# Attention over six nodes: the value product in two column halves, projections in the gap between them, the q edge folded into Wq, the residual summed in PSUM

## The reference, cut to what matters

```python
for c in range(NUM_NOD):                       # 6 nodes, D = 128, H = 8 heads of 16
    nsrc = min(c + 1, MAX_PREV)
    snode = c - nsrc
    eq, ek, ev = (lind + nsrc - 1, lind, lind + nsrc // 2)
    in_q, in_k, in_v = (c - 1, snode, snode + nsrc // 2)
    q = ew[c, 0] * (nodes[in_q] @ We[eq] + be[eq])
    k = ew[c, 1] * (nodes[in_k] @ We[ek] + be[ek])
    v = ew[c, 2] * (nodes[in_v] @ We[ev] + be[ev])
    o = _mha(q, k, v, Wq[c], Wk[c], Wv[c], Wo[c])   # softmax((q Wq)(k Wk)^T / 4) (v Wv) Wo
    nodes[c] = act_w[c] * o + q
    lind += nsrc
out = nodes[NUM_NOD - 1]
return _layernorm(out, ln_g, ln_b)
```

## Time and profile before

| what | value |
|---|---|
| runs shown | 2585.63, 2601.75 and 2603.72 us, median 2601.75 |
| the profiled execution | 2587.72 us, of which the span of the trace is 2585.9 |
| PE busy | 2319.4 us, 90% |
| DVE busy | 2235.8 us, 86% |
| ACT busy | 1781.2 us, 69% |
| mean granted TensorE clock | 0.959 |

### The profile page before, as it was taken

The page is one execution under the profiler, slowest core; times in us unless marked ns, Lnnn a source line. Parts: engine busy times, 40 slices in busy tenths (PEclk is TensorE's granted clock), DMA queues, the critical chain, the costliest instruction groups (busy, mean ns, idle before and its releaser), DMA issues.

```text
span 2585.9 us, 39227 instructions
## 1 busy us (share of the span) xinstructions
PE 2319.4 (90%) x13473; PEld 869.1 (34%) x13473; DVE 2235.8 (86%) x3998; ACT 1781.2 (69%) x3417; POOL 115.0 (4%) x74
## 2 busy tenths in 40 slices
PE   6588989999999999999999999999999999999996
PEld 3233333333333333333333333333333333333331
DVE  7488788899989999899999999999899899898982
ACT  3136567777777777777777777777777777767773
POOL 1000000000000000000000000000000000010110
PEclk8679899999999999999999999999999999999995
DMA  3404133242253243253243243243243243143311
GB/s 90 108 21 83 39 74 79 54 115 77 60 114 75 62 114 76 61 115 80 58 114 81 57 105 85 46 105 83 47 105 87 44 105 89 42 104 88 65 29 33
DMA packets 93262, 198.46 MB, mean 77 GB/s; under 512 B 26115, under 2 KB 43799, under 8 KB 93063
## 3 DMA queue, kind: packets, MB, share of 16 engines
q1 hardware_dynamic: 93062, 195.96, 32.4%
HBM read 116.65 MB, written 64.42 MB: 70 GB/s over the span
## 4 chain that ended last, share of the span: by engine, by line
PE 63%; DVE 14%; ACT 11%; DMA 6%; issue 4%; SPq 2%; ACTq 0%; POOL 0%; POOLq 0%; DVEq 0%
PE bank L511 25%; PE bank L464 22%; ACT e_ring L670 10%; DVE max_half L963 9%; PE bank L484 5%; DMA q_aug<-max_part 5%; PE bank L312 2%; PE bank L323 2%; PE bank L342 2%; SPq L1167 2%; PE bank L331 1%; PE bank L257 1%; PE bank L350 1%; ACT raw L680 1%; PE bank L258 1%
## 5 line engine op out<-in xcount | busy, mean ns | idle before, releaser
L963 DVE TENSOR_REDUCE max_half<-bank 128x1 f32<-128x512 f32 x3072 | 1924.3, 682 | 257.1 <-PE bank L484 243.4
L670 ACT ACTIVATE e_ring<-bank 128x512 f32<-128x512 f32 x3072 | 1610.9, 601 | 609.7 <-PE bank L464 609.4
L464 PE MATMUL bank<-q_aug,k_aug 50*128 50x512 f32 x3072 | 1142.0, 453 | 159.0 <-ACT e_ring L670 149.7
L484 PE MATMUL bank<-k_aug,q_aug 48*128 48x512 f32 x3072 | 1153.0, 456 | 48.2 <-DMA q_aug<-part_dram 25.7
L464 PEld LDWEIGHTS bank<-q_aug,k_aug 50*128 50x128 f32 x3072 | 503.2, 188 | 1209.9 <-ACT e_ring L670 1113.0
L511 PE MATMUL bank<-e_ring,v_aug 128*32 128x512 f32 x6144 | 836.7, 617 | 0.0
L484 PEld LDWEIGHTS bank<-k_aug,q_aug 48*128 48x128 f32 x3072 | 500.8, 188 | 84.9 <-DVE max_half L963 49.6
L511 PEld LDWEIGHTS bank<-e_ring,v_aug 128*32 128x32 f32 x6144 | 121.7, 108 | 206.4 <-ACT e_ring L670 117.9
L1030 POOL TENSOR_TENSOR ctxT<-ctxT,rden_bc 128x1024 f32<-128x1024 f32 x23 | 54.6, 2375 | 1938.9 <-DMA rden_bc<-rden_dram 1938.8
L680 ACT ACTIVATE raw<-bank 128x512 f32<-128x512 f32 x96 | 57.4, 598 | 27.9 <-PE bank L511 26.0
L331 PE MATMUL bank<-node_ring,w_q 128*128 128x512 f32 x96 | 56.2, 670 | 3.1 <-DVE k_part L805 0.7
(11 more groups left out here) (167 smaller groups left out, 687.8 us busy)
## 6 DMA issues: line engine op xcount, KB each, us to landing
part_dram<-k_part SPq DMA_DIRECT2D x24, 1024.0 KB, 4.0
k_aug<-part_dram SPq DMA_DIRECT2D x48, 512.0 KB, 10.1
part_dram<-q_part SPq DMA_DIRECT2D x24, 1024.0 KB, 5.0
q_aug<-part_dram SPq DMA_DIRECT2D x48, 512.0 KB, 13.4
src<-node_dram SPq DMA_DIRECT2D x40, 512.0 KB, 3.4
k_aug<-part_dram SPq DMA_DIRECT2D x48, 256.0 KB, 8.1
q_aug<-part_dram SPq DMA_DIRECT2D x48, 256.0 KB, 14.4
q_aug<-max_part SPq DMA_DIRECT2D x768, 2.0 KB
```

Of the source, the lines that this page charges most:

```text
L464: e.matmul(bank[i][:, :], k_aug[first:first + AUG, u % 2, h // 2, chunk * P:(chunk + 1) * P].bitcast(F32R), q_aug[first:first + AUG, u % 2 ...
L484: e.matmul(bank[i][:, :], q_aug[first:first + SPLIT, u % 2, h // 2, q0:q0 + P].bitcast(F32R), k_aug[first:first + SPLIT, u % 2, h // 2, ha ...
L670: e.activation(e_ring[:, n % E_SLOTS, :], bank[i][:, :], ACT.Exp, scale=EXP_SCALE).then_inc(a_exp, 1)
L963: e.tensor_reduce(max_half[:, G % 2, row, kh:kh + 1], bank[MAX_BANKS[ring % 3]][:, :], AX_X, ALU.max).then_inc(v_mx, 1)
```

## The change

- **Value product.** In a step in which PE has no side product, the value product is issued in two halves of 256 columns: the first before the last pair of score and maxima products, the second after it. In a step with a side product, that product takes the place ahead of the last pair and the value product stays whole, at the end.
- **Side products.** At most one in a step. `project_q` is gone: We[eq] is folded into Wq in the prologue (`fold`), and qh comes straight from the node. Each output projection now begins with the edge product of the node (`project_node`, accumulated in bank 7), and `project_out` adds Wo's product on top, so PE does 10 in a unit again, at r = 0, 1 (qh), 4, 5 (kh), 12 to 15 (node and output, twice) and 24, 25 (v). ACT evicts the sum with one bias (`evict_out`); DVE's `add_out` is gone. The bias of v is carried through Wo (`out_biases`), so DVE's eviction of v is a plain copy.
- **Parts of q and k.** ACT evicts the unrounded value, and POOL rounds it and subtracts (`split`, two instructions of 128x512 each, four times a unit). DVE's `rest_k` and `rest_q` are gone.
- **Maxima.** The transpose moves from r % 8 = 2 to r % 8 = 3 and from the ring of maxima banks to bank 7; DVE's negation follows at the end of that step.
- **SP.** The order of the list within a unit changes: q's store and loads come first (r = 3, 5, 6), k's store and loads after the denominators (r = 7, 9, 10), and the source of v moves from r = 23 to r = 11.

```diff
+        QH_AT, KH_AT, OUT_AT, TURN_AT, V_AT = (0, 1), (4, 5), (12, 13, 14, 15), (16, 17), (24, 25)
...
             def head_q(u, hf, at):
                 c, b = divmod(u, B)
                 where["qh", u, hf] = at
                 bk = free_bank(at)
-                e.wait_ge(a_q, 2 * u + hf + 1)
-                e.matmul(bk[:, :], w_q[:, c, :], node_ring[:, b, (c + 1) % 2, half_of(hf)], start=True, stop=True).then_inc(p_qh, 1)
-                freed[at] = (v_qr, 2 * u + hf + 1)
+                wait_node(u)
+                e.matmul(bk[:, :], w_q[:, c, :], node_ring[:, b, c % 2, half_of(hf)], start=True, stop=True).then_inc(p_qh, 1)
+                freed[at] = (a_q1, 2 * u + hf + 1)
...
+            def project_node(u, hf):
+
+                c, b = divmod(u, B)
+                bk = free_bank(MISC)
+                e.matmul(bk[:, :], w_edge_q[:, c, :], node_ring[:, b, c % 2, half_of(hf)], start=True, stop=False)
+
             def project_out(u, hf):
                 c, b = divmod(u, B)
-                bk = free_bank(MISC)
                 e.wait_ge(g_norm, u + 1)
-                e.matmul(bk[:, :], w_o[:, c, :], ctxT[:, half_of(hf)], start=True, stop=True).then_inc(p_o, 1)
-                freed[MISC] = (v_oa, 2 * u + hf + 1)
+                e.matmul(bank[MISC][:, :], w_o[:, c, :], ctxT[:, half_of(hf)], start=False, stop=True).then_inc(p_o, 1)
+                freed[MISC] = (a_oa, 2 * u + hf + 1)
...
+            def turn_maxima(G):
+                bk = free_bank(MISC)
+                e.wait_ge(v_cmb, G + 1)
+                e.transpose(bk[0:NR, 0:P], max_col[:, G % 2, :], ident[:, :]).then_inc(p_turn, 1)
+                freed[MISC] = (v_neg, G + 1)
+
+            def weighted(z, columns, first, last):
...
+                if first:
+                    e.wait_ge(a_exp, HG * z + HG)
...
+                for j in range(HG):
+                    done = e.matmul(bank[CTX_BANK][j * VW:(j + 1) * VW, columns], v_aug[:, u % 2, chunk, hg * HG + j, :],
+                                    e_ring[:, (HG * z + j) % E_SLOTS, columns], start=(chunk == 0 and first),
+                                    stop=(chunk == NCH - 1 and last))
+                if last:
+                    done.then_inc(p_ctx, 1)
...
             for s in range(-LOOKAHEAD, LAST_STEP):
+                product = product_of(s)
+                late = late_stages(s)
+                z = s - 1
                 for j in range(HG):
...
+                    if j == HG - 1:
+                        if product:
+                            product()
+                        elif 0 <= z < STEPS:
+                            weighted(z, slice(0, BANK // 2), True, False)
                     if 0 <= s < STEPS:
...
+                        scores(s, j)
...
+                        maxima(m)
                 if 0 <= z < STEPS:
...
+                    if product:
+                        weighted(z, slice(0, BANK), True, True)
+                    else:
+                        weighted(z, slice(BANK // 2, BANK), False, True)
+                for i, k in late:
+                    mix(i, k, lambda: MISC)
...
+            def evict_out(u, hf):
...
+                e.activation(node_ring[:, b, (c + 1) % 2, half_of(hf)], bank[MISC][:, :], ACT.Identity,
+                             bias=col[:, C_BO + c:C_BO + c + 1]).then_inc(a_oa, 1)
...
+            def split(part, hf, signal_to):
+                x, high = part[:, 1, half_of(hf)], part[:, 0, half_of(hf)]
+                after()
+                step(e.tensor_copy(high.bitcast(F32R), x))
+                after()
+                signal(e.tensor_tensor(x, x, high, ALU.subtract), signal_to)
...
             def store_k(u):
-                e.wait_ge(v_kr, 2 * u + 2)
+                e.wait_ge(g_k, 2 * u + 2)
...
             def store_q(u):
-                e.wait_ge(v_qr, 2 * u + 2)
+                e.wait_ge(g_q, 2 * u + 2)
...
                     if 1 <= nxt < UNITS:
-                        k = r - shift_of(nxt)
                         if r == 0:
                             load_source(nxt, 0)
-                        if k == 6:
+                        if r == 3:
+                            store_q(nxt)
+                        if r in (5, 6):
+                            load_aug(nxt, 0, r - 5)
+                        if r == 7:
                             store_k(nxt)
-                        if k == 8:
-                            store_q(nxt)
-                        if k in (8, 9):
-                            load_aug(nxt, 1, k - 8)
-                        if k in (11, 12):
-                            load_aug(nxt, 0, k - 11)
-                        if r == 23:
+                        if r in (9, 10):
+                            load_aug(nxt, 1, r - 9)
+                        if r == 11:
                             load_source(nxt, 1)
```

More of the change, by code:

```diff
@@ L304, in wait_node @@
                 else:
[L305 to L313, removed]
+                    e.wait_ge(a_oa, 2 * (u - B) + 2)
             def head_k(u, hf, at):
@@ L370, in last_turn, with scores @@
                 freed[MISC] = (a_last, hf + 1)
-            def stages(s, half):
+            def scores(s, j):
+                n = HG * s + j
+                G, chunk = divmod(s, NCH)
+                u, g = divmod(G, GPU)
+                hg, qh = divmod(g, NHALF)
+                h = hg * HG + j
+                i = ST_BANKS[n % 3]
+                if n >= 3:
+                    e.wait_ge(a_exp, n - 2)
+                elif i in freed:
+                    e.wait_ge(*freed[i])
+                if j == 0 and chunk == 0:
+                    if g == 0 and u < 2:
+                        e.wait_ge(d_ones[u], DMA * 2)
+                    e.wait_ge(d_max_in[G % 2], DMA * 2 * HG * (G // 2 + 1))
+                first = (h % 2) * ROWS
+                e.matmul(bank[i][:, :],
+                         k_aug[first:first + AUG, u % 2, h // 2, chunk * P:(chunk + 1) * P].bitcast(F32R),
+                         q_aug[first:first + AUG, u % 2, h // 2, half_of(qh)].bitcast(F32R),
+                         start=True, stop=True).then_inc(p_st, 1)
@@ new lines, in maxima @@
+            def maxima(m):
+                G, t = divmod(m, NCH * HG)
+                u, g = divmod(G, GPU)
+                hg, qh = divmod(g, NHALF)
+                hj, qt, kh = max_tile(t)
+                h = hg * HG + hj
+                first = (h % 2) * ROWS
+                q0 = qh * BANK + qt * P
+                i = MAX_BANKS[m % 3]
+                if m >= 3:
+                    e.wait_ge(v_mx, m - 2)
+                elif i in freed:
+                    e.wait_ge(*freed[i])
+                if t == 0 and g == 0:
+                    e.wait_ge(d_aug, AUG_ALL * (u + 1))
+                e.matmul(bank[i][:, :], q_aug[first:first + SPLIT, u % 2, h // 2, q0:q0 + P].bitcast(F32R),
+                         k_aug[first:first + SPLIT, u % 2, h // 2, half_of(kh)].bitcast(F32R),
+                         start=True, stop=True).then_inc(p_mx, 1)
@@ L400, in tensor_program @@
+                return None
             e.wait_ge(g_ident, 1)
@@ L405, in tensor_program @@
             e.wait_ge(a_wt, 7)
+            edges = [raw_w[:, WE_KV + n, :] for n in range(2 * NODES)] + [w_edge_q[:, c, :] for c in range(NODES)]
             misc_turn = [0]
@@ L1048, in stages @@
                 nxt, prev = u + 1, u - 1
+                if 1 <= nxt < UNITS and half == 1:
+                    if r in QH_AT:
+                        split_q(nxt, r - QH_AT[0])
+                    if r in KH_AT:
+                        split_k(nxt, r - KH_AT[0])
                 if 0 <= prev < LAST:
@@ L1079, in gpsimd_program @@
                     mix(i, k)
+                z = t - UNIT0_AT
+                if z == 1:
+                    for hf in range(NHALF):
+                        split_k(0, hf)
+                    for hf in range(NHALF):
+                        split_q(0, hf)
             e.wait_ge(p_mt2, EARLY)
@@ L1123, in load_aug @@
                         e.wait_ge(d_part_k, DMA * (u + 1))
+                    else:
+                        e.wait_ge(d_part_q, DMA * (u + 1))
+                    if u == 0 or side == 0:
                         if u == 0:
@@ L1129, in load_aug @@
                             e.wait_ge(p_st, HG * UC * (u - 1))
-                    else:
-                        e.wait_ge(d_part_q, DMA * (u + 1))
                 first = parity * ROWS
```

399 lines of the change are left out of this document (158 added, 241 removed).

## The result

The changed kernel takes 2692.92 us (median of 4 runs, 2686.83 to 2704.39), the kernel before beside it 2602.73 (4 runs). The ratio is 1.0365, with a 95% interval of 1.0308 to 1.0422: slower, and 33 us beyond the upper end of the range that was predicted.

The account below looks back on a forecast made before the run. The DMA queue was taken to bound steps 4 to 16, PE and DVE the rest; 21 units at -4.6 + 4.2 + 1.3 = +0.9 give +19, with -7 +12 on 2587.7: 2600 us, range 2465 to 2660.

Parts of the forecast that it names:

- Clock: Behind the 5 us stop before step 16: 3.4 us at half clock, costing 1.3 us a unit, bounds 0 and 2.6.
- the sum: Twenty-one units at -4.6 + 4.2 + 1.3 = +0.9 give +19, with -7 that is +12 on 2587.7: 2600 us.
- the half clock stays longer: Rival: 6.8 us of half clock after each 5 us stop, and longer loads: 2627 to 2669 us; 27 in 100.
- The first stretch: Steps 4 to 16 of a unit, set by the DMA queue: 41.1 us against 36.9, plus 4.2; bounds 38.5 and 43.5.
- the walk: SP's DMA list followed issue by issue from step 4: denominators land at 18.1, k's store 25.8, step 16 starts at 41.1.
- the first rival: The denominators' store passes q's loads in the queue, step 16 isn't held: unit 91.2, total 2467 us; 15 in 100.
- POOL's scaling: Between steps 4 and 16: done at about 27 us, wanted by step 13 at 26.9, so nothing more lost.
- The second stretch: Step 16 to the next unit's step 4, 20 steps set by PE and DVE: 55.1 us against 59.7, minus 4.6.
- A half: Half a value product on PE in a step without a side product: 0.56 us, bounds 0.50 and 0.75.
- PE's need from T4 to T16: PE's own time from step 4 to step 16 without the DMA queue: 36.1 us.
- Small terms: Prologue minus 3 us by an earlier first maxima product; units 0 and 1 minus 4 together; the end left as is.

Follow-up runs that it names:

- experiment 5: Changed kernel with denominators and k's store before q's loads, src load at r = 21, second half of k's loads behind step 16's maxima: 2437.19 us, ratio 0.9397.
- experiment 2: Changed kernel plus five unused 128x128 by 128x512 products on PE ahead of step 16 in every unit, inside the stop: 2588.47 us, ratio 0.9971.
- experiment 3: Changed kernel with the value product whole at the end of every step, all else kept: 2698.06 us, ratio 1.0377.
- experiment 6: Changed kernel with the value product whole in steps 16, 17 and 18 as well, its SP order kept: 2630.94 us, ratio 1.0159.
- experiment 7: Kernel before, with value product halves in steps without a side product and q's last two loads behind step 16's maxima: 2479.45 us, ratio 0.9572.
- experiment 4: Kernel before, with only the value product halved in steps without a side product: 2648.39 us median of ten runs; ratio 1.0047 from the four shortest.

## Why the prediction was wrong

**The step of it that failed is "Clock": "I count 1.3 a unit; bounds 0 and 2.6."** It is a term of the sum that was mis-sized, by a factor of nearly five. Steps 16 to 23 take 26.91 us in the changed kernel and 20.67 in experiment 5, where there is no half clock: 6.2 a unit, and 104 us in all by experiment 2. The working took the length of the half clock from one place, 3.4 us behind a stop of 1.4, and priced it in plain steps. What the runs showed in its place is 18.1 us a unit at half clock. The price of a microsecond at half clock was about right, 1.3 / 3.4 = 0.38 us in the working and 6.2 / 18.1 = 0.34 as measured; it is the length that failed. The rival named after this, "the half clock stays longer", had the direction, but gave it 6.8 us, and so ended at 2669 at most, longer loads included. Had I taken 6.2 in place of 1.3, the sum would have come to 2600 + 21 x 4.9 = 2703.

Why it is so long, couldn't tell, and no row could: before, PE was not stopped for 5 us at such a place. Behind such stops even whole value products have 8.6 us (experiment 3), and halves more. What the runs show is that the length depends on what PE does behind the stop (experiments 3 and 6, with stops of 5.2 and 5.4 us). Why it does stays open.

**The first stretch** was walked rightly. Measured from T4 in the unit above: denominators stored at 8.4, landed at 18.6 (18.1 in the walk), broadcasts issued by 22.2 (21.7), k's store landed at 26.4 (25.8). The store did wait behind q's loads, so the first rival fell at once. In the mean it is 42.27 against 41.1, inside the bounds; +5.3 a unit where +4.2 stood. What is missing lies in the queue: by the timelines of the 19 units k's store lands 27.1 us after PE starts step 4 in the mean, where the walk had 25.8, and PE starts step 16 14.9 behind that, where it had 15.3. POOL's scaling came later than the walk had it, and PE waits 12.5 us for it in sum, some 0.5 a unit. It costs no time here: it stands ahead of the stop, and a DMA releases step 16 either way.

```profile
L357 PE MATMUL bank<-ctxT,w_o 128*128 128x512 f32 x92 | 51.8, 645 | 12.7 <-POOL ctxT L1032 12.5
```

**The second stretch** was right to the tenth, in part by luck. 20.67 + 34.41 = 55.1 at full clock (experiment 5), as in the sum. But from first exponential to first exponential (medians over the units) steps 19 and 27, with the negated maxima, take 2.75 and 2.76 where 3.05 stood, step 3 takes 2.75 where 2.55 stood, the 13 plain steps take 33.2 together where 32.9 stood, ACT's 0.4 included (2.47 or 2.48 in seven of them, 2.76 in steps 21 and 29), and the four side product steps 13.6 where 13.5 stood. These errors cancel. A half is 0.57 where 0.56 stood, and two halves cost 0.14 more than a whole one of 1.00. The Trainium skill (TensorEngine Tiling (Array Packing), section Key Properties) says that a change of tiling mode drains the engine. The 0.14 may be that; no run here takes it apart, and it takes off a part of the gain and no more. PE's need from T4 to T16, 36.1 in the sum, is 35.8.

**Small terms.** The first exponential comes 1.8 us earlier (3 in the sum). Units 0 and 1 gained 18.5 us together, where I had 4, and the rest (the start of unit 2 and all behind unit 20) gained 5, where the sum had units 21 and 22 lose 2. Why units 0 and 1 gain so much wasn't tested. With the clock at +94 (19 x 4.9) and the queue at +21 (19 x 1.1) these make up the 93 us between 2600 and the profiled execution.

**What the change is worth.** Of the 6.0% of experiment 5, halves and the shorter queue make up 4.3% in the old stages (experiment 7); side products spread over the unit, the lighter DVE and the rest add 1.7%. Between the spans of experiments 7 and 5 that is 48.6 us: 20 of them in units 2 to 20, 18 in units 0 and 1, the others at the ends. All of it was there in the changed kernel as it stood, hidden by the order of SP's list, where a small store stood behind 1.5 MB of loads.

## What to carry to other kernels

- Before a change that makes steps shorter, ask what PE will meet at the next place at which it waits for a DMA: a faster step can turn a queue that is just in time into a stop. In the old stages the halving of the value product changed the time by +0.5% (by +1.9% in the median of all runs) or by -3.8%, by whether two more loads stood ahead of eight small DMAs.
- Price a stop of PE by its length plus the half clock behind it, and don't take that clock's length from one stop elsewhere in the trace. Filling a stop with useless products is a cheap experiment that tells the two apart.
- In a list that stops at each wait, put the store whose landing is waited for ahead of the large loads, and the DMA that releases PE between them.

## What was new about the hardware

- The granted clock stayed at half while PE worked. In experiment 4 the profile has PE busy for 47.80 of 47.80 us (the ends of matmuls are modelled in it) with the clock at 0.50. The Trainium skill (TensorE: Matmul & The Clock Gate, section What's actually happening) has the clock set by how busy PE has been recently, half when it was idle and full when it was busy. These rows don't agree with that for the work in question, steps of pairs and column halves. Halves don't bar the rise either: in the changed kernel it came in steps 17 and 18, behind halves alone, in 7 of the 19 units.
- With stops of 5.2 to 5.6 us in the mean, the half clock a unit was 18.1 us with halves behind it up to step 18, 10.6 with three whole value products there and 8.6 with whole ones throughout. At full clock the same halves never lost it: experiments 5 and 7 have none in units 2 to 20. What in a whole value product lets the clock rise isn't settled: a half has shorter products and more changes of tiling, and these weren't taken apart.
- The length of a stop doesn't say what follows. In one profile (experiment 4) a stop of 1.91 us was followed by 47.8 us of half clock and one of 2.17 by none. In the changed kernel the shortest stop of units 2 to 20, 4.72 us, has the longest half clock behind it, 34.1 us, and one of 5.88 the shortest, 10.2. In the unit of experiment 2 shown above, stops of 0.27 and 1.34 with products between them were followed by none. So a mean over many units is needed.
